# Edge slots of a two-layer graph network: cells counted in blocks, bases by mask products on chip, ranks ahead of the normalisations, first normalisation applied by ScalarE

## The reference

```
deg = maximum(segment_sum(ones, dst, 1250), 1)
xn = layernorm(x)
x = x + gnn0(xn, src, dst, deg) + mix0(xn)        # mix0: flow attention + feed-forward, normalised again inside
x = x + ffn0(layernorm(x))
xn = layernorm(x)
x = x + gnn1(xn, edge_index, edge_weight) + mix1(xn)
x = x + ffn1(layernorm(x))                        # 8 experts, 2 of them taken for each node
```

## Time and profile before

| | us |
|---|---|
| median of three runs | 2168.05 (2165.76 to 2168.8) |
| profiled execution, its own time | 2162.18 |
| its span in the trace | 2160.4 |
| TensorE, matmuls busy | 1702.7 (79%) |
| VectorE busy | 887.1 (41%) |
| GpSimd busy | 745.5 (35%) |
| ScalarE busy | 551.2 (26%) |
| scatter of the edges (GpSimd, L339), busy | 306.3 |

### The profile page before, as it was taken

How to read it: one execution, slowest core, us unless ns; L and a number is a source line. 1 busy time by engine, 2 the same in 40 slices (tenths; PEclk the granted TensorE clock), 3 DMA queues, 4 the chain that set the end, 5 groups by cost and what they waited for, 6 DMA issues and landing times. The chain is left out here.

```text
span 2160.4 us, 26017 instructions
## 1 busy us (share of the span) xinstructions
PE 1702.7 (79%) x7775; PEld 1076.7 (50%) x7776; DVE 887.1 (41%) x2087; ACT 551.2 (26%) x1476; POOL 745.5 (35%) x838
## 2 busy tenths in 40 slices
PE   5533212228889978888897999979999999999998
PEld 4111001003354656666544444557777777777775
DVE  7900000004663689999897565660000000000002
ACT  0000000001013469999311111332221221122222
POOL 0677777740000079999820221012000000007004
PEclk9976556558889999999998999979999999999999
DMA  7000000000800020000204000457450440042003
GB/s 220 2 2 2 2 2 2 2 1 20 330 29 15 25 68 1 0 0 0 50 0 136 1 0 0 156 206 250 155 204 15 175 175 19 19 170 67 19 19 105
DMA packets 76227, 143.88 MB, mean 67 GB/s; under 512 B 21809, under 2 KB 23425, under 8 KB 71941
## 3 DMA queue, kind: packets, MB, share of 16 engines
q1 hardware_dynamic: 49415, 118.27, 15.6%
q0 software_dynamic: 18976, 10.95, 2.2%
q10 hardware_dynamic: 7776, 13.97, 2.0%
HBM read 107.58 MB, written 35.53 MB: 66 GB/s over the span
## 5 line engine op out<-in xcount | busy, mean ns | idle before, releaser
L339 POOL DMA_INDIRECT sorted_edges<-fa_records,fa_edge_slot x313 | 306.3, 978 | 156.8 <-issue 101.5
L2092 PEld LDWEIGHTS et_ps_h<-ex_turned,arena 128*128 128x128 f32 x3072 | 348.6, 193 | 17.1 <-issue 17.1
L2092 PE MATMUL et_ps_h<-ex_turned,arena 128*128 128x128 f32 x3072 | 348.8, 276 | 5.9 <-issue 5.9
L2102 PE MATMUL et_ps_y<-arena,et_hidden_t 128*128 x768 | 337.5, 592 | 0.0
L2002 DVE TENSOR_SCALAR ex_turned<-et_ps_t,ex_ln_g,ex_ln_b 128x128 f32<-128x128 f32 x96 | 32.8, 405 | 583.9 <-PE et_ps_t L2072 583.9
L1083 POOL TENSOR_SCALAR ad_row<-iota,ad_edges 128x128 fp32r<-128x128 f32 x392 | 270.1, 708 | 2.8 <-DMA ad_edges<-sorted_edges 2.8
L2102 PEld LDWEIGHTS et_ps_y<-arena,et_hidden_t 128*128 128x128 f32 x768 | 142.2, 190 | 160.7 <-issue 160.7
L1973 POOL DMA_INDIRECT xn_rows<-slot_out,from_slots x10 | 12.2, 1218 | 475.3 <-POOLq L1970 472.6
L1150 PE MATMUL ad_ps<-ad_to,ad_row_high 128*128 128x320 f32 x392 | 139.0, 362 | 46.1 <-ACT ad_row_low L1131 46.0
L1130 ACT ACTIVATE ad_row_high<-ad_row,ad_edges 128x128 fp32r<-128x128 f32 x392 | 155.1, 396 | 25.7 <-POOL ad_row L1083 6.5
L1109 DVE TENSOR_TENSOR arena<-arena,ad_ps 128x640 f32 x196 | 158.2, 807 | 3.3 <-PE ad_ps L1151 3.3
(11 more groups left out here) (398 smaller groups left out, 2154.9 us busy)
## 6 DMA issues: line engine op xcount, KB each, us to landing
arena<-L_ffn_W SPq DMA_DIRECT2D x16, 4096.0 KB, 18.8
slot_rows<-fa_zeros SPq DMA_DIRECT2D x1, 7424.0 KB, 26.3
slot_out<-fa_zeros SPq DMA_DIRECT2D x1, 7168.0 KB, 45.4
slot_out<-et_y ACTq DMA_DIRECT2D x24, 256.0 KB
et_rows_in<-slot_rows ACTq DMA_DIRECT2D x24, 256.0 KB
sorted_edges<-fa_records,fa_edge_slot POOLq DMA_INDIRECT x313
arena<-x SPq DMA_DIRECT2D x1, 2240.0 KB
neighbour<-fa_Wv SPq DMA_DIRECT2D x10, 224.0 KB
```

Source lines behind the costliest of these rows:

```text
L339: nc.gpsimd.indirect_dma_start(g.sorted_edges, bass.IndirectOffsetOnAxis(ap=self.edge_slot[0:rows, e:e + 1], axis=0), self.records[0:rows, ...
L2092: last = pe.matmul(ps_h[:, f % 2, i, :], x.weights[:, at:at + P], turned[:, k, :], start=(k == 0), stop=(k == KD - 1))
L2102: last = pe.matmul(ps_y[:], hidden_t[:, i, :], x.weights[:, bass.ds(buffer * (2 * HALF) + (HALF + i * D), D)], start=(i == 0), stop=(i == ...
```

## The change

Five things are changed, all in `flow_attention` and `Positions`.

1. **Columns and blocks.** The edge tile gets 324 columns, in 27 blocks of 12. The one-hot tile is laid out by block: `[128, 27, 40*12]`, so that a block of all buckets is contiguous. Each of the 40 comparisons writes 27 runs of 12.
2. **Counting.** A cell is now (bucket, column in the block), 480 of them, taken as four quarters of 10 buckets, 120 cells on 120 partitions. One product for each quarter and block (108 in all, with weights of 120 columns) gives the counts as `[120, 4, 27]`. The first may start when the first quarter's one-hots are written.
3. **Bases.** Running sums over blocks are made on VectorE; sums over the columns of a block and over the buckets are made by products with masks of 120 by 120, which GpSimd makes (17 constants in place of 9). The bases stay on chip as `[120, 2, 4, 27]`; they get into PSUM by products with a column of them as broadcast weights and the identity as the moving tile, two for each quarter. A bank thus takes nine matmuls in place of two. The way through DRAM (`move_bases`) is gone. The table `group_offset` is made last.
4. **Units and order.** The ranks are made in eight units: 12, 36, five times 48, and 36 columns (the scatter needs 25 of them). VectorE makes bases and the first seven units ahead of the statistics of `n1`. The nine comparisons for the source's block become a multiplication and a shift of integers.
5. **First normalisation.** ScalarE applies it (`Identity` with a scale and a bias `lift`), and VectorE takes the statistics of `n2` tile by tile behind it. On SP's queue the fill goes ahead of x.

```
+BANK = 12
+EP = -(-EDGES // (P * BANK)) * BANK
+UNITS = [(0, 0, 1), (0, 1, BANKS)] + [(n, 0, min(BANKS, BLOCKS - n * BANKS)) for n in range(1, -(-BLOCKS // BANKS))]
...
         for b in range(NB):
-            last = v.tensor_scalar(self.hot[r, b, :], self.bucket[r], float(b), None, ALU.is_equal)
-        last.then_inc(s["hot_made"], 1)
+            last = v.tensor_scalar(self.hot[r, :, b * BANK:(b + 1) * BANK], self.bucket[r].rearrange("p (k e) -> p k e", k=BLOCKS),
+                                   float(b), None, ALU.is_equal)
+            if b % QUARTER == QUARTER - 1:
+                last.then_inc(s["hot_made"], 1)
...
     def count(self, pe, g):
-        for e in range(EP):
-            last = pe.matmul(self.ps_total[:, e:e + 1], self.hot[0:P, :, e], self.ones[0:P, 0:1], start=True, stop=True)
+        for q in range(QUARTERS):
+            pe.wait_ge(s["hot_made"], q + 1)
+            for k in range(BLOCKS):
+                last = pe.matmul(self.ps_count[:, q, k:k + 1], self.hot[0:P, k, q * CELL:(q + 1) * CELL],
+                                 self.ones[0:P, 0:1], start=True, stop=True)
+        last.then_inc(s["counted"], 1)
+        pe.wait_ge(s["cumulated"], 1)
+        pe.matmul(self.ps_total, self.same, self.upto[:, :, BLOCKS - 1], start=True, stop=True).then_inc(s["totalled"], 1)
+        pe.matmul(prefix, self.same, self.upto.rearrange("p q k -> p (q k)"), start=True, stop=False)
+        pe.wait_ge(s["negated"], 1)
+        pe.matmul(prefix, self.from_own, self.minus.rearrange("p q k -> p (q k)"), start=False, stop=True)
+        pe.wait_ge(s["grouped"], 2)
+        pe.matmul(self.ps_first, self.from_bucket, self.own_groups, start=True, stop=False)
+        pe.matmul(self.ps_first, g.ones[0:CELL, 0:CELL], self.groups_upto, start=False, stop=True)
+        pe.wait_ge(s["base_made"], 1)
+        pe.wait_ge(s["past_made"], QUARTERS)
+        for i, (n, first, last) in enumerate(UNITS):
+            for j in range(first, last):
+                bank = self.ps[0:P, n % 2, j, 0:NB * BANK]
+                pe.matmul(bank, self.before[0:P, 0:P], self.hot[0:P, n * BANKS + j], start=True, stop=False)
+                for q in range(QUARTERS):
+                    for h in range(2):
+                        base = self.base_h[:, h, q, n * BANKS + j:n * BANKS + j + 1]
+                        placed = pe.matmul(bank[:, q * CELL:(q + 1) * CELL], base.broadcast_to([CELL, P]),
+                                           self.ident_h[0:CELL, 0:CELL], start=False, stop=(h == 1))
+            placed.then_inc(s["placed"], 1)
...
             positions.mark(nc, dve, c)
-            positions.record(nc, dve, c, g)
-            dve.wait_ge(g.x_loaded, 32)
+            positions.record_weights(nc, dve, c)
+            positions.bases(nc, dve, c, g)
+            positions.count_groups(nc, dve, g)
+            positions.record_places(nc, dve, c)
+            positions.ranks(nc, dve, c, range(len(UNITS) - 1))
+            dve.wait_ge(g.x_loaded, 16 * len(ROW_CUTS))
             n1.all_stats(nc, c, g.x)
             n1.variance(nc, c)
-            positions.bases(nc, dve, c, g)
-            with c.rounds(T // 2, 2) as j:
-                for u in range(2):
-                    t = j * 2 + u
-                    c.step(n1.apply(nc, tile(g.xn, t), tile(g.x, t), t))
+            v.scalar_tensor_tensor(lift[r], n1.mean[r], -1.0, n1.rstd[r], ALU.mult, ALU.mult).then_inc(s["lifted"], 1)
+            positions.ranks(nc, dve, c, [len(UNITS) - 1])
+            for t in range(T):
+                dve.wait_ge(s["normed"], t + 1)
+                c.step(v.bn_stats(tile(n2.stats, t), tile(g.xn, t)))
             c.settle()
-            n2.all_stats(nc, c, g.xn)
             n2.variance(nc, c)
-            positions.ranks(nc, dve, c, g)
+            positions.take_table(nc, dve, c, g)
...
         def _(act):
             n1.root(nc, act)
-            positions.move_bases(act, g.edge_base)
+            for t in range(T):
+                act.wait_ge(s["lifted"], 1)
+                nc.scalar.activation(tile(g.xn, t), tile(g.x, t), ACT.Identity, bias=column(lift, t),
+                                     scale=column(n1.rstd, t)).then_inc(s["normed"], 1)
```

More of the change, by code:

```diff
@@ L280, in __init__ @@
         self.records, self.edge_slot = m.sb("records", [P, EP, 4]), m.sb("edge_slot", [P, EP], U32)
[L281 to L287, removed]
         self.slot_i = m.sb("slot_i", [P, 2, SECTION], I32)
         self.ps = banks.rearrange("p (u j) n -> p u j n", u=2)
[L290 to L293, removed]
+        self.ps_count, self.ps_prefix = (banks[0:CELL, bank, 0:QUARTERS * BLOCKS].rearrange("p (q k) -> p q k", q=QUARTERS)
+                                         for bank in (4, 6))
+        self.ps_total, self.ps_first = banks[0:CELL, 5, 0:QUARTERS], banks[0:CELL, 7, 0:QUARTERS]
+        self.ps_table = banks[0:1, 4, 0:NG]
+        names = ("padded dst_loaded loaded made filled zeroed hot_made counted cumulated negated totalled prefixed grouped offset "
+                 "past_made tabled base_made placed taken slots_made chain")
         self.s = {n: m.sem("po_" + n) for n in names.split()}
-    def section(self, a, n, j):
-        at = n * SECTION + j * BANK
-        return a[:, :, at:at + BANK]
     def load(self, sp, A, g):
@@ L365, in record @@
[L365 to L371 removed]
+        c.step(v.tensor_copy(self.src_f[r], self.src_i[r]))
@@ L401, in ranks @@
[L401 to L409 removed]
+        c.link(v.tensor_copy(g.group_offset[0:1, :], self.table))
@@ new lines, in ranks @@
+    def ranks(self, nc, dve, c, units):
+        s, v, r = self.s, nc.vector, slice(0, P)
+        for i in units:
+            n, first, last = UNITS[i]
+            size = (last - first) * BANK
+            at = slice(n * SECTION + first * BANK, n * SECTION + last * BANK)
+            dve.wait_ge(s["placed"], i + 1)
+            chosen = self.chosen[r, 0:last - first]
+            v.tensor_tensor(chosen, self.ps[r, n % 2, first:last, 0:NB * BANK], self.hot[r, n * BANKS + first:n * BANKS + last],
+                            ALU.mult).then_inc(s["taken"], 1)
+            dve.wait_ge(s["taken"], i + 1)
@@ L430, in count @@
-        pe.matmul(self.ps_first, g.before[0:NB, 0:NB], self.groups[:], start=True, stop=True).then_inc(s["offset"], 1)
-        pe.wait_ge(s["past_made"], 1)
-        pe.matmul(self.ps_table, g.ones[0:NB, 0:1], self.past, start=True, stop=True).then_inc(s["tabled"], 1)
-        pe.wait_ge(s["base_loaded"], 16)
-        for n in range(SECTIONS):
-            pe.wait_ge(s["taken"], n + 1 if n > 1 else 2)
-            for j in range(BANKS):
-                out = self.ps[0:P, n % 2, j, 0:NB * BANK].rearrange("p (b e) -> p b e", b=NB)
-                pe.matmul(out, self.before[0:P, 0:P], self.section(self.hot[0:P], n, j), start=True, stop=False)
-                last = pe.matmul(out, self.ones[0:2, 0:P], self.section(self.base_row, n, j), start=False, stop=True)
-            last.then_inc(s["placed"], 1)
+        pe.wait_ge(s["made"], MADE)
@@ L443 @@
+        pe.wait_ge(s["taken"], len(UNITS) - 1)
+        for q in range(QUARTERS):
+            last = pe.matmul(self.ps_table, self.first_row, self.past[:, q, :], start=(q == 0), stop=(q == QUARTERS - 1))
+        last.then_inc(s["tabled"], 1)
 class Shared:
```

215 lines of the change are left out of this document (127 added, 88 removed).

## The result

The changed kernel is slower: 2190.59 us median of five runs (2181.51 to 2193.04) against 2168.56 (2165.76 to 2170.54), ratio 1.0098, interval 1.0077 to 1.0118. The forecast was 2144 us; the rival that ends on the slower side, "the stretch swallows the ranks", is what happened, at a sixth of its price. The profiled execution took 2189.84 us (span 2188.0), 27.7 more than that of before.

The account below looks back on a forecast made before the run. Bound: a slow stretch beside the edge scatter, 1.40 us per TensorE instruction, ending with it. Scatter 31.9 us earlier, less 3.1 and 4.8, nets 24.0: 2138.2 against 2162.18, stated as 2144 for the median; range 2130 to 2160.

Parts of the forecast that it names:

- the stretch swallows the ranks: Rival, chance 0.11: rank instructions behind the scatter's start are held at 1.40 us each, scatter starves, time 2310.
- The chain up to the scatter: One-hots, counting, bases and first unit in `flow_attention`: scatter starts at 28.1 in place of 59.97, 31.9 us earlier.
- The slots never hold it up: Later rank units take VectorE 6.5 us each and the scatter 62, so the scatter never waits for slots.
- TensorE's tiles at 90.2: Start of TensorE's projection tiles, behind units, statistics and normalisations: 90.2 us in place of 101.59.
- the sum: Net gain of the stage: 31.9 - 3.1 - 4.8 = 24.0 us.
- If the stretch ends with the scatter, the scatter's start sets the time: End of `flow_attention`: an earlier scatter start moves the kernel's time one for one, 31.9 us earlier.
- the stretch: About 112 to 492 us, beside the edge scatter in `flow_attention`: TensorE's signals come at 1.40 us an instruction.
- 3.1 and 4.8 us: Losses at the projections: 14.6 fewer instructions through by the stretch's end, 3.1; part of the lead ahead of the pace, 4.8.
- the store: Guess within the rival: about 100 unanswered TensorE instructions fill up before the pace sets in.

Follow-up runs that it names:

- d_mult: Changed kernel with bases placed by one product a bank, VectorE making the moving tile, `group_offset` comparisons behind the second unit: 2155.36 us, 0.9947 of the kernel before.
- b_half2: Kernel before with every second column of edges left out, 156 scatters in place of 313: 1982.27 us with the stretch.
- b_split4_2: Kernel before with each rank product cut in four by columns, 512 rank instructions in place of 128: 2223.58 us with the stretch.
- c_spread: Changed kernel with bases placed by one product a bank in place of eight, 162 rank instructions for 486: 2153.5 us with the stretch, 1844.85 without.

## Why the prediction was wrong

- **The chain up to the scatter: right.** 28.83 for 28.1; each step within 0.9 us, the bank at 1.2 us, below the 1.6. The comparisons took 230 ns each (9.22 us for 40) for 154 before; the half speed that was forecast gives 240, one number at a time would give 405.
- **The step that failed:** the ranks behind the first unit were costed at 6.5 us a unit, "The slots never hold it up", and TensorE's tiles at 90.2 followed from it. The same text had read off that every TensorE instruction takes 1.40 us while the scatter runs, and applied that in its sum only to the tiles' 560. The runs show four units let through, the fourth already 8 us late, then 100.80 us a unit: the last was taken at 412.95 where the sum has 73.4, the tiles began at 443.87, and the slots did hold the scatter up, twice.
- **"If the stretch ends with the scatter, the scatter's start sets the time": right as to the end, not as to the whole.** VectorE took its last late projection at 467.60 instead of 492.99, 25 us earlier (31.9 forecast). The scatter's own lead shrank from 31.1 us at its first issue to 17.0 at its last; the two waits for slots, 5.7 and 12.8 us before 344.85 and 418.31, are more than that, and the other DMAs took some 4 us less. In d_mult and b_half2 too the stretch ended behind the last scatter, by 28 us (469.62) and 18 (277.27).
- **What that step cost.** From 468.44 to the end of the last projection at 566.15 TensorE still had 97.7 us of projections to do, in place of 41.7 from 493.73 on the earlier trace rows: 56.0 us more, some 262 instructions at 0.214. It began on them 25.3 earlier (468.44 for 493.73), so the last projection is 30.7 later. The sum had 3.1 and 4.8 us for this. At the end of the kernel 27.7 are left by the two profiled executions and 22.0 by the medians; the profiled one of before lay 6 us under its median.
- **The rival.** Its pace was right to the microsecond (101 us a unit), and the starving of the scatter came too; the store is still a guess. Its price of 142 us was off by two terms. It counted 468 rank instructions behind the scatter's start, but TensorE had run four more banks of 18 by then: 396 were left. Its store of 100 was too small: 28.83 + (396 - x) times 1.40 = 412.95 gives 122 (the same sum in b_split4_2, with 372 left at 59.92 and the last section taken at 416.82, gives 117). So 543 for the last unit became 412.95, and the starving 18.5 us in two waits. A chance of 0.11 was too low for a rule that I had measured myself.
- **One thing no trace of before could show:** that the stretch is a condition of the set of runs. The forecast's gain is real without it, -23.4 us for -24.0, but for another reason than the sum gave: there the scatter's end releases `adjacency`. That the two numbers agree is luck.

## What to carry to other kernels

A pace that is charged for each instruction applies to all that is issued while it lasts: when you move a long transfer ahead, first list what now falls beside it, counted in instructions and not in microseconds. In this kernel 358 more TensorE instructions undid an earlier start of 31 us, with the stretch; without it they cost nothing that shows. And run the kernel before beside each experiment: here one edit (holding the scatter) moved the distance to it by 18 us to the better in one condition and by 38 to the worse in the other, and only fewer instructions (c_spread) gained in both.

## What was unexpected of the hardware

- The kernel before took 2160 to 2171 us in four sets and 1865 to 1872 in two. The gap of 300 us is the slow stretch. It is no property of a chip: one chip gave both in different sets.
- Within the stretch a TensorE instruction costs 1.40 us on the mean of loads and matmuls, which always came in pairs here (2.80 a pair), with 100 columns or 512 (89.6 for 64, 100.8 for 72, 22.4 for 16). VectorE and ScalarE show it too: the statistics of L228 came 2.80 and 5.60 us apart, and in c_spread2 ScalarE's instructions of L453 started at 56.15, 57.55, 58.25, 59.65, 61.75 and 63.15, all multiples of 0.70 apart.
- A signal lagged its instruction far: the last rank product ran at 324.75 and was answered at 412.95, 88.2 us or 63 instructions at 1.40 (in b_split4_2 328.54 and 416.82, 88.3 us). The Trainium skill, "Advanced Engine Details and Errata", Engine Queue Depths, gives TensorE a queue of 64; the lag agrees with that number, and no run here shows that it is this queue.
- What the indirect DMAs do to the other engines stays open. The Trainium skill, "NOTIFIC — the notification-queue block", section on overflow ("three behaviours, one of which stalls the engine"), says that the internal pipeline of this block, which the page names as the transport under instruction tracing and profiling, holds its producers back rather than lose a record. That would fit a store of some 120 instructions followed by a fixed price for each; no run here shows it.
- A rival that no run here tests: every execution on record, the timed ones too, lists a span and a granted clock, so none is known to have run without the profiler. Whether the stretch, and with it the loss of 22 us, would be there without it stays open.
